# Rounding the bf16 parts of queries and keys on DVE in place of ACT, in a hybrid layer kernel whose engines follow written lists

## What is computed

```
x = x + attention(layernorm(x))      # 16 heads of 8, elu(q)+1, elu(k)+1
x = x + moe_ffn(layernorm(x))        # 8 experts of 512, top 2, and a shared one
x = x + mamba(layernorm(x))          # width 256, 16 states, a scan over the tokens
x = x + moe_ffn(layernorm(x))
# in the attention, with rope only in the numerator:
q = elu(q) + 1; k = elu(k) + 1; rot_q = rope(q); rot_k = rope(k)
weights = (rot_q @ rot_k.T) / (q @ k.T)
out = weights @ v
```

## Time and profile before

| | us |
|---|---|
| three runs: lowest, median, highest | 3748.87, 3752.46, 3768.64 |
| the profiled execution | 3761.18 |
| its span, first to last instruction | 3759.4 |
| PE busy in the span | 3412.8 (91%) |
| ACT busy | 3189.4 (85%) |
| DVE busy | 2658.9 (71%) |
| POOL busy | 1330.1 (35%) |
| mean granted clock of PE, share of 2.4 GHz | 0.949 |

### The profile page before, as it was taken

One profiled execution on the slowest core, in us unless ns is written; L12 is line 12 of the kernel. 1 busy time (PEld: TensorE's weight loads), 2 busy tenths in 40 slices (PEclk: granted clock), 3 DMA queues, 4 the chain that ended last, 5 costly groups with the idle time before them and its releaser, 6 DMA issues. The chain is left out here.

```text
span 3759.4 us, 38374 instructions
## 1 busy us (share of the span) xinstructions
PE 3412.8 (91%) x11446; PEld 1450.4 (39%) x11446; DVE 2658.9 (71%) x3527; ACT 3189.4 (85%) x4024; POOL 1330.1 (35%) x744
## 2 busy tenths in 40 slices
...
GB/s 161 122 84 110 138 152 157 140 179 134 178 136 163 163 132 182 128 196 138 159 151 147 174 134 178 143 159 151 140 174 138 182 146 163 149 108 165 117 128 76
DMA packets 214847, 552.01 MB, mean 147 GB/s; under 512 B 25105, under 2 KB 96626, under 8 KB 214642
## 3 DMA queue, kind: packets, MB, share of 16 engines
...
...
## 5 line engine op out<-in xcount | busy, mean ns | idle before, releaser
L938 PE MATMUL bank<-hF,wst 128*128 128x512 f32 x2304 | 1149.6, 620 | 30.4 <-ACT hF L1040 15.6
L1525 POOL TENSOR_TENSOR yM<-yM,ws 128x1024 f32<-128x1024 f32 x240 | 634.3, 2643 | 1410.4 <-DVE ws L1422 1407.2
L1303 DVE TENSOR_TENSOR rPool<-bank,rPool 128x512 f32<-128x512 f32 x1024 | 700.1, 686 | 550.4 <-PE bank L866 440.5
L1040 ACT ACTIVATE hF<-bank,cols 128x512 f32<-128x512 f32 x1152 | 772.3, 687 | 259.4 <-PE bank L927 245.3
L1194 ACT ACT_TABLE_LOAD x518 | 664.6, 1283 | 9.2
L1040 ACT ACTIVATE rPool<-bank 128x512 f32<-128x512 f32 x1024 | 571.9, 597 | 93.9 <-PE bank L861 87.5
L925 PE MATMUL bank<-xnH,wst 128*128 128x512 f32 x1152 | 605.4, 526 | 30.7 <-ACT hF L1040 20.2
L1415 DVE TENSOR_TENSOR_SCAN ws<-dAs,ws 128x1024 f32<-128x1024 f32 x256 | 600.9, 2353 | 7.4 <-ACT dAs L1040 0.8
L938 PEld LDWEIGHTS bank<-hF,wst 128*128 128x128 f32 x2304 | 419.9, 193 | 463.5 <-issue 364.2
L866 PE MATMUL bank<-qpk,kpk 48*128 48x512 bf16 x1024 | 412.2, 405 | 94.0 <-DVE rPool L1303 85.7
L1040 ACT ACTIVATE rPool<-rPool 128x2048 f32<-128x2048 f32 x256 | 490.4, 1916 | 2.3
(11 more groups left out here) (162 smaller groups left out, 2934.6 us busy)
## 6 DMA issues: line engine op xcount, KB each, us to landing
...
bc<-bcscr SPq DMA_DIRECT2D x256, 512.0 KB, 4.4
cB<-gscr SPq DMA_DIRECT2D x256, 256.0 KB, 4.6
kpk<-kscr SPq DMA_DIRECT2D x128, 192.0 KB, 5.5
qpk<-qscr SPq DMA_DIRECT2D x128, 192.0 KB, 5.9
...
```

Source lines behind the costliest of these rows:

```text
L938: pe.matmul(ps[FFN][:, :], w2, hF[:, (NCH * f + q) % HSLOTS, :], start=(c == 0), stop=(c == FC - 1)).then_inc(s_dn, 1)
L1040: return nc.scalar.activation(out_, in_, fn, **kw)
L1303: v.tensor_tensor(rP[:, slot, c, :], ps[num_bank(b, s)][:, :], rP[:, slot, c, :], ALU.mult).then_inc(s_mul, 1)
L1525: g.tensor_tensor(yM[:, :, :], yM[:, :, :], ws[:, s % 3, :, :], ALU.add).then_inc(s_ya, 1)
```

## The change

The function `cast` stays on ACT for batch 0 only. For all other batches the same rounding is a `tensor_copy` on DVE, with the same three waits. All the lists are new ones: DVE's have the casts, ACT's have them no longer, and steps of all engines have changed places. In `MAIN` some twenty steps move by one or two places on PE, five on ACT besides the casts, few on the others. In `FINISH` the orders differ widely, and ACT's has 117 table loads for 108.

```
@@ -1083,10 +1085,10 @@
                 elif name == "cast":
                     t, part = divmod(n, 2)
                     slot = t % 2
-                    act.wait_ge(s_A_rope, floor(6 * b + 3 * (t // 2) + 3))
-                    act.wait_ge(s_A_split, floor(16 * b + 2 * n))
+                    act.wait_ge(s_A_rope, 3 * (t // 2) + 3)
+                    act.wait_ge(s_A_split, 2 * n)
                     if part == 0:
-                        act.wait_ge(s_pk[slot], floor(N_PK * (2 * b + t // 2)))
+                        act.wait_ge(s_pk[slot], N_PK * (t // 2))
                     a(parts[:, slot, part, :], til[:, t, :], ACT.Copy).then_inc(s_A_split, 1)
 
             def att(b, name, n):
@@ -1270,6 +1272,14 @@
                     v.wait_ge(s_A_relu, floor(4 * b + n + 1))
                     v.wait_ge(s_A_exp, floor(4 * b + n + 1))
                     v.scalar_tensor_tensor(til[:, n, :], eA[:, n % 2, :], 1.0, til[:, n, :], ALU.min, ALU.add).then_inc(s_A_til, 1)
+                elif name == "cast":
+                    t, part = divmod(n, 2)
+                    slot = t % 2
+                    v.wait_ge(s_A_rope, floor(6 * b + 3 * (t // 2) + 3))
+                    v.wait_ge(s_A_split, floor(16 * b + 2 * n))
+                    if part == 0:
+                        v.wait_ge(s_pk[slot], floor(N_PK * (2 * b + t // 2)))
+                    v.tensor_copy(parts[:, slot, part, :], til[:, t, :]).then_inc(s_A_split, 1)
                 elif name == "rope":
                     if n == 0:
                         v.wait_ge(s_wearly, 16 * N_EARLY)
```

The lists of ACT, DVE and POOL for the iterations 3 to 13:

```
     "ACT": """
-    T.gelu H.gelu*2 T.log A.ln*4 N.decay A.ex T.gelu H.gelu*2 F.mean H.gelu*6 T.log A.ln N.decay A.ln*2 F.var A.ln*2
-    A.ex N.decay T.gelu H.gelu*2 T.log A.ln F.router N.decay T.gelu F.gelu*4 T.log A.ln*2 H.close P.load A.ln*2 A.ex
-    P.mean A.ln*2 N.decay P.var N.decay T.gelu F.gelu*6 T.log A.ln*2 P.qk A.ex A.ln*2 P.qk A.ex N.decay T.gelu
-    F.gelu*6 T.log A.ln*4 P.qk A.ex A.ln*3 N.decay A.ln N.decay A.ln A.ex T.gelu F.gelu*6 P.cast F.gelu*2 T.log
-    A.ln*2 P.qk T.gelu F.gelu*2 P.cast F.gelu T.log A.ln E.mean A.ex A.ln*3 E.var A.ln T.gelu F.gelu*2 P.cast
-    F.gelu*3 T.log A.ex A.ln G.mean A.ln P.cast G.var A.ln T.gelu F.gelu*4 T.log A.ln G.router T.gelu G.gelu*4
-    P.cast G.gelu M.mean T.log M.var A.ex M.xp A.ln*2 M.xp T.gelu G.gelu*2 M.xp G.gelu*2 T.silu M.silu*2 M.xp P.cast
-    M.silu*2 M.row T.log A.ln*2 M.dt A.ex A.ln M.dt A.ln M.sp A.ln T.gelu G.gelu T.log M.decay A.ln M.decay A.ex
-    A.ln*5 A.ex M.decay T.gelu G.gelu*4 P.cast G.gelu*2 T.log A.ln*2 M.decay*2 A.ln A.ex T.gelu G.gelu*2 P.cast
-    G.gelu*2 T.log A.ln*4 A.ex A.ln*4 A.ex T.gelu G.gelu*4 T.log M.decay*2 A.oT
+    T.gelu H.gelu*2 T.log A.ln*3 N.decay A.ln A.ex T.gelu H.gelu*2 F.mean H.gelu*6 T.log A.ln N.decay A.ln*2 F.var
+    A.ln*2 A.ex N.decay T.gelu H.gelu*2 T.log F.router A.ln N.decay T.gelu F.gelu*4 T.log A.ln*2 H.close P.load
+    A.ln*2 A.ex P.mean A.ln*2 N.decay P.var N.decay T.gelu F.gelu*6 T.log A.ln*2 P.qk A.ex A.ln*2 P.qk A.ex N.decay
+    T.gelu F.gelu*6 T.log A.ln*4 P.qk A.ex A.ln*3 N.decay A.ln N.decay A.ln A.ex T.gelu F.gelu*8 T.log A.ln*2 P.qk
+    T.gelu F.gelu*3 T.log A.ln E.mean A.ex A.ln*3 E.var A.ln T.gelu F.gelu*5 T.log A.ex A.ln G.mean A.ln G.var A.ln
+    T.gelu F.gelu*4 T.log A.ln G.router T.gelu G.gelu*5 M.mean T.log M.var A.ex M.xp A.ln*2 M.xp T.gelu G.gelu*2
+    M.xp G.gelu*2 T.silu M.silu*2 M.xp M.silu*2 M.row T.log A.ln*2 M.dt A.ex A.ln M.dt M.sp A.ln*2 T.gelu G.gelu
+    T.log M.decay A.ln M.decay A.ex A.ln*5 A.ex M.decay T.gelu G.gelu*6 T.log A.ln M.decay*2 A.ln*2 A.ex T.gelu
+    G.gelu*4 T.log A.ln*4 A.ex A.ln*4 A.ex T.gelu G.gelu*4 T.log M.decay*2 A.oT
 """,
     "DVE": """
     A.v H.part F.mean A.mul N.dbx A.mul*2 N.scan N.hc A.mul H.part N.dbx N.scan F.var N.hc A.mul H.part F.router
     A.mul F.route N.dbx H.part N.dbx A.mul F.turn N.scan N.hc A.mul P.mean A.mul N.scan A.mul N.dbx N.hc P.var
     F.part A.mul N.scan N.dbx N.scan N.hc F.part A.mul*2 N.hc A.mul*4 N.dbx P.til N.scan A.mul N.dbx P.til N.hc
-    A.mul*3 F.part A.mul*2 N.scan A.mul*2 N.hc F.part N.dbx N.scan N.hc A.mul*3 F.part P.til E.mean F.part P.til
-    A.mul*3 E.var E.gate F.part G.mean A.mul*2 F.part G.var G.router G.route F.part G.turn M.mean A.mul*2 M.var
-    A.mul M.conv*2 A.mul M.conv*6 A.mul*2 G.part A.mul*5 M.dt M.dbx*2 M.scan M.hc A.mul G.part A.mul M.scan A.mul*2
-    M.dbx M.scan M.hc*2 A.mul G.part A.mul*3 M.dbx*2 M.scan A.mul M.hc A.mul*2 G.part A.mul M.scan A.mul*3 M.hc
-    A.mul*2 G.part A.mul*2 M.dbx A.mul M.dbx M.scan*2 M.hc*2 A.close
+    A.mul*3 F.part A.mul*2 N.scan A.mul*2 N.hc F.part N.dbx P.cast N.scan N.hc A.mul*3 P.til F.part E.mean P.cast
+    P.til F.part A.mul*3 E.var P.cast E.gate F.part G.mean A.mul P.cast A.mul F.part G.var G.router G.route F.part
+    G.turn P.cast M.mean A.mul*2 M.var A.mul M.conv*3 A.mul M.conv*5 A.mul P.cast A.mul G.part A.mul*5 M.dt M.dbx*2
+    M.scan M.hc A.mul G.part A.mul M.scan A.mul*2 M.dbx M.scan M.hc P.cast M.hc A.mul G.part A.mul*3 M.dbx*2 M.scan
+    A.mul P.cast M.hc A.mul*2 G.part A.mul M.scan A.mul*3 M.hc A.mul*2 G.part A.mul*2 M.dbx A.mul M.dbx M.scan*2
+    M.hc*2 A.close
 """,
     "POOL": """
-    H.add N.acc*2 H.add*3 N.acc*5 F.add P.rope F.add N.acc*2 P.rest F.add*2 P.rest*2 P.rope P.rest F.add*3 M.take
-    P.rest*2 M.keep M.acc P.rest G.add P.rest M.acc G.add M.acc*2 G.add*2 M.acc*2 P.keep
+    H.add N.acc*2 H.add*3 N.acc*5 F.add P.rope F.add N.acc*2 P.rest F.add*3 P.rest*2 P.rope P.rest F.add*2 M.take
+    P.rest*2 M.keep M.acc P.rest G.add P.rest M.acc*2 G.add M.acc G.add*2 M.acc*2 P.keep
 """,
 }
```

PE's list around the M part, before and after:

```
-    A.av A.num A.den*2 A.num*2 A.den G.up A.num G.down*2 G.up*2 A.den*2 A.av G.down*2 A.den A.num A.den*2 G.down*2
-    A.den A.num*2 A.av A.num G.up*4 G.down*2 A.num A.den G.up A.den A.num G.up A.num A.av G.down*3 A.num G.up*2
...
+    A.av A.num M.dt A.av A.num A.den*2 A.num*2 G.up A.num G.down A.den G.down G.up*2 A.den*2 A.av G.down*2 A.den
+    A.num A.den*2 G.down*2 A.den A.num*3 A.av G.up*4 G.down*2 A.num G.up A.den*2 A.num G.up A.num A.av G.down*3
```

More of the change, by code:

```diff
@@ new lines @@
+    0:A.num*3 0:A.den 0:A.num*2 0:A.den*2 0:A.num 0:A.den*3 0:A.av*2 0:A.den 0:A.num*2 0:A.den*2 0:A.num 0:A.den
+    0:A.av 0:A.den*2 0:A.num*2 0:A.den*2 0:A.num*3 0:A.den 0:A.num 0:A.den 0:A.num*3 0:A.av*2 0:A.num*3 1:A.den
+    0:A.av 1:A.v 1:A.den 0:A.close 1:F.mean 1:A.num 1:A.den*3 1:F.var 1:A.den*3 1:F.router 1:F.up*4 1:A.num 1:F.up*2
+    1:F.down*2 1:F.turn 1:A.num 1:F.down 1:A.num 1:F.down 1:A.num 1:A.den*2 1:A.num 1:P.load 1:F.up*3 1:P.mean
+    1:F.up 1:F.down 1:A.den*2 1:F.down*3 1:A.num 1:A.av 1:A.den 1:F.down 1:F.up 1:A.den*2 1:P.var 1:A.num 1:F.up
@@ new lines @@
+    2:A.num*2 2:F.var 2:A.den*4 2:A.num*2 2:F.router 2:A.av 2:A.den*3 2:A.num 2:A.den 2:A.num 2:F.up*2 2:A.num
+    2:F.up*2 2:F.turn 2:P.load 2:A.den*2 2:P.mean 2:F.down 2:A.den*2 2:A.num*2 2:F.down*2 2:P.var 2:A.av 2:A.den
+    2:A.num 2:A.den 2:F.down 2:F.up*7 2:P.qk 2:F.down*3 2:A.num 2:A.den 2:F.down 2:A.den 2:P.qk 2:A.num 2:F.down
+    2:A.num 2:A.den*2 2:F.down 2:P.qk 2:A.num 2:A.av 2:A.num 2:F.up 2:A.num 2:F.up*4 2:A.num 2:F.down*2 2:F.up
+    2:A.den*2 2:A.num 2:A.av 2:A.num 2:P.qk 2:A.den*2 2:A.num 2:A.av 2:A.num 2:A.den*2 2:F.up 2:A.num 2:F.down
@@ L96 @@
+    2:G.down*2 2:A.den 2:A.num 2:A.den*2 2:A.num*2 2:G.down*2 2:A.num 2:A.av 2:A.num 2:G.up*2 2:A.num 2:G.up 2:A.num
+    2:G.up 2:A.av*2 2:A.close
 """,
@@ L144 @@
+    2:A.mul*3 2:G.part 2:A.mul 2:M.scan 2:A.mul*3 2:M.hc 2:A.mul*2 2:G.part 2:A.mul*3 2:M.dbx*2 2:M.scan*2 2:M.hc*2
+    2:A.close
 """,
@@ L157 @@
+    G.w*2 M.bc*2 G.gate G.w P.pk G.w G.gate*2 M.bc*2 P.ahead*2 G.gate G.w
 """,
     "PE": """
[L159 to L162 removed]
@@ new lines @@
+    A.den*2 F.var A.den A.av A.num A.den*2 H.up*2 A.den H.down*4 F.router A.den A.num H.down*4 A.num F.up*2 A.den
+    F.up*2 F.turn A.num H.close P.load A.den*2 P.mean A.den*2 A.num F.down*2 P.var A.num A.av F.up A.den*2 A.num
+    F.down*2 F.up*5 P.qk F.down*4 A.den F.up A.den A.num P.qk A.num F.down A.num F.down P.qk A.den*2 A.num A.av
+    A.num F.up A.num F.up*4 A.num F.down F.up F.down A.den*3 A.num A.av A.num P.qk A.den A.num A.av A.den A.num
+    A.den F.up A.num F.down A.den*2 A.num F.down*3 A.num A.den A.av A.num F.up*5 F.down F.up*2 F.down F.up F.down
@@ L338 @@
[L338 to L341 removed]
+    14:A.mul 14:N.scan 14:N.dbx 14:N.hc 14:N.scan 14:F.part 14:A.mul*2 14:N.hc 14:A.mul*3 14:N.dbx*2 14:A.mul
@@ new lines @@
+    14:N.scan 14:P.til*2 14:A.mul 14:N.hc 14:A.mul 14:F.part 14:A.mul*4 14:N.scan 14:A.mul*2 14:N.hc 14:F.part
+    14:P.cast 14:N.dbx 14:N.scan 14:A.mul 14:N.hc 14:A.mul*2 14:F.part 14:E.mean 14:P.til*2 14:P.cast 14:A.mul
+    14:F.part 14:A.mul*2 14:E.var 14:P.cast 14:E.gate 14:P.cast 14:F.part 14:G.mean 14:A.mul*2 14:F.part 14:G.var
+    14:G.router 14:A.mul 14:G.route 14:F.part 14:G.turn 14:M.mean 14:A.mul*2 14:M.var 14:A.mul 14:M.conv*3 14:A.mul
```

(1 more changed line is left out.)

429 lines of the change are left out of this document (202 added, 227 removed).

## The result

The changed kernel takes 3833.1 us in the median of four runs (3814.9 to 3841.5), against 3752.1 us of the kernel before on the same chip. The ratio of the runs is 1.0203, 95% interval 1.0176 to 1.0229. By the medians that is slower by 81 us (by the ratio 76) where 22 were forecast, and above the range. The profiled execution took 3835.1 us (span 3833.2), 74 more than that of before, and the profile is read against it.

What follows compares the result with a forecast made beforehand. PE was taken as the bound. Twelve iterations +24 us, first attention iteration -3 and closing list +1 made +22 on the median 3752.5: 3774 us, +0.6%, range 3740 to 3792.

Steps and rivals of the forecast that it cites:

- ACT's relief: Casts leaving ACT, 5.0 us per iteration: gain bounded by 0 and 2.5 us per iteration, taken as 0.4.
- Rival B: ACT was the hidden bound and the new lists use its 5.0 us: -32, 3720 us; chance 0.14.
- A cast on DVE: Priced from the rounding L1311 of the same shape: 0.427 us, possibly 0.4 to 0.69; eight make 3.4 us per iteration.
- Cast 6: Between two hc on DVE, M part: POOL goes in between, mul starts 2.8 us later, PE loses 2.4 per iteration.
- cast 4: One of casts 1 to 5, in front of steps before which DVE sits idle: claimed to cost nothing.
- Rival A: The blocked hc is covered, so PE does not wait for it: -7, 3746 us; chance 0.25 together with D.
- Casts 0 to 5 and 7: DVE's other casts: 1 to 5 in idle gaps, 0 where PE has no wait, 7 before an hc; each taken as 0.
- Rival C: POOL catches more than cast 6, a second 2.4 us stall at cast 7 or the scan: 3803 us; chance 0.14.
- The new order of PE: Iterations' order nearly that of before, some twenty items moved by one or two; reordering taken as 0.
- The prediction's last sign of being wrong: The forecast also fails if the new lists give another neighbour of mul the time of the stall.
- The sides: Outside the iterations: -3 us in the first attention iteration, 0 in the next, +1 in the closing list.
- sign that the prediction had named for being right: hc about 3.6 us, L866 wait over 2 us, PE idle 11 to 12 us per iteration, ln and hF waits hardly smaller.

Runs made afterwards that it cites:

- e11: Kernel before, casts of MAIN's eleven iterations moved from ACT to DVE, cast 6 behind mul 49 and cast 4 behind mul 34: 3754 us, ratio 1.0002.
- e6: Kernel before, only the casts of MAIN's eleven iterations moved from ACT to DVE, at the changed kernel's places: 3787 us, ratio 1.0098.
- e2: Changed kernel, cast 6 in MAIN moved on DVE from between two hc steps to behind mul 49: 3811 us, ratio 1.0165.
- e14: Changed kernel, MAIN with PE's list and ACT's order of before, cast 6 behind mul 49, cast 4 behind mul 34: 3767 us, ratio 1.0065.
- the fillers: Matmuls nobody reads, put in PE's waits: five per iteration in the kernel before, 3729 us; fourteen in the changed kernel, 3794 us.
- e4: Kernel before with the changed kernel's MAIN lists of PE, DVE, POOL and SP, casts and ACT's list as before: 3823 us, ratio 1.0194.

## Why the prediction was wrong in size

1. *PE bounds, and ACT's relief is worth 0.4 us per iteration.* Right but for the 0.4, of which e11 shows nothing. Rival B, ACT as the hidden bound, is refuted by it.
2. *A cast on DVE takes 0.427 us.* It takes 0.418 in the median.
3. *Cast 6: hc about 3.6 us, mul 2.8 or 2.5 later, PE loses 2.4.* Right: 3.37, 2.49, and a wait of 2.3; in e6 2.5 us more idle time per iteration, 0.5 of them cast 4's. Rival A, a covered hc, is refuted. By the Trainium skill (SBUF — State Buffer, on its two separate sides) a POOL step that reads SBUF and a DVE step that uses both ports or has two inputs in SBUF block each other for a whole instruction; the trace agrees, and again POOL went in between the cast and the hc.
4. *Casts 0 to 5 and 7 cost nothing.* Wrong for cast 4, 0.5 us per iteration. Looking at DVE's gaps alone overlooked that the harm is done to POOL's step beside it, which PE waits for. Rival C was of this kind, with the wrong place and price.
5. *The new order of PE is nearly that of before; 0.* This is the step that failed. "Some twenty items change places by one or two" was counted and not walked through. Two adjacent items, num 48 and av 11, put 0.88 us of wait on PE, and num 37 another 0.72. Put at 0, it was worth about 39 us in the changed kernel (e2 to e14, cast 4's place included). The prediction's last sign of being wrong, a new neighbour of mul that gets the time of the stall, names this case, but the sum has no term for it.
6. *A term that was not there.* Every us of the sum was idle time. The 6.8 us more at half clock per iteration stand for 3.4 us in the books, beside the idle time's 2.4; how much of that would stay without the added waits is not known, and the fillers show 1.2 of it. None of the rivals had it, though the earlier trace rows has the clock at 0.99 and the trace of before has its half clock right behind pairs of waits.
7. *The sides, -3 and +3 (iteration 14 and tail).* Measured 0 and +11 (17 by the ratio). The -3 was to come from waits for ln in the first attention iteration; they went from 9.5 to 7.8 us in the profile, and 1.7 us can't be told where the length varies by 11.

Nearly every sign that the prediction had named for being right came: an hc of 3.37 us, PE idle 12.2 us per iteration in the twelve, waits for ln hardly smaller. All of these are about idle time, so they could come while the time was 59 us off.

The parts don't add up as single prices: the order beside ACT's old list 73, the casts alone 35, the closing lists 11, all together 81. One overlap is seen: where the clock is halved behind num 48, the ups and downs last longer, and num 49 waits only 0.84 to 1.2 us behind cast 6 in place of 2.3. Also, num 57 and up 63 wait in e4 and don't in the changed kernel. How much of the rest of the overlap is the clock's was not separated.
